# Attention maxima carried to the query rows by DMA from GpSimd's tiles, with queries strided over the score tiles

## The chip, the cores and the metric

The kernel runs on one core of a Trainium2 chip. The metric is device time in microseconds (us) for one launch. Engines are called as the profile calls them: PE (TensorE, with its weight loads as PEld), DVE (VectorE), ACT (ScalarE), POOL (GpSimd), and SP (SyncE), which here only issues DMAs.

## What is computed

A Mamba layer with residual and layer norm, and then a second layer that adds 16-head attention and a top-2 mixture of eight experts, with residual and layer norm. Batch is 8, length 1024, width 256, head width 16. The change touches the attention alone:

```python
qkv = (x @ W_qkv + b_qkv).reshape(B, S, 3, H, hd)
q, k, v = (qkv[:, :, 0], qkv[:, :, 1], qkv[:, :, 2])
attn = jnp.einsum('bqhd,bkhd->bhqk', q, k) / jnp.sqrt(jnp.asarray(hd, x.dtype))
attn = jax.nn.softmax(attn, axis=-1)
attn_out = jnp.einsum('bhqk,bkhd->bqhd', attn, v).reshape(B, S, D)
```

## The kernel before

`mamba_phase` runs first, for all eight batches; `attention_phase` follows and takes the second half of the time. Each engine runs its own instructions in the order in which they are written; semaphores tie them.

For each batch the attention phase has an expert stage (`experts`) and then sixteen head steps (`step(b, h, ...)`). Per head every score is computed twice. First `scores` (L1242) multiplies a 128-query tile `qt` of `q_st`, as the stationary operand, by all 1024 keys, in two halves; DVE's `take_max` (L1623) reduces each tile to the negated row maximum, `neg_max[:, h % 2, qt]`. Later `scores_t` (L1281) multiplies a 128-key tile `kt` of `k_st`, stationary, by the queries of one half, moving. This product has two rows more: `q_st` holds the negated maxima in two float16 parts, `k_st` a constant, so that the maximum is subtracted by the matmul. ACT's `exp_unit` (L1509) turns the result into `probs`, and `weigh_v` (L1296) multiplies these by V.

`q_st` and `k_st` hold each head twice, at partitions 0 and 64. A `scores_t` of one half is issued beside a `scores` of the other half, so the two run in different rows of the PE array.

A step of head h on PE has eight units, kt = 0 to 7. Each issues `scores_t(h, kt, 0)`, `scores(h + 2, kt, 1)`, `scores_t(h, kt, 1)`, `scores(h + 2, kt, 0)` and then `weigh_v`: tiles 4 to 7 of head h - 1 in units 0 to 3, tiles 0 to 3 of head h in units 4 to 7 (LAG = 4). Below, (kt, half) names a `scores_t` or its exponential. Steps 14 and 15 have no `scores`; in their place come parts of the next batch's projections. `turn_o` (L1311), in unit 5, transposes the weighted sums of head h - 1, which ACT's `take_o` (L1516) has copied out of PSUM bank 6; DVE's `normalise` divides them. `weigh_v(h, 0)`, in unit 4, overwrites bank 6 and so waits for `take_o`.

Three PSUM banks (RING = 4, 5, 7) go round among users in a fixed order, the list USERS: the sixteen (kt, half) of a head, `rows` after (3, 1), and `sums` (`turn_o`) after (5, 1). A user waits in `ring_free` until the user three places before it has been read.

The maxima's path from `neg_max` to `q_st`, for head h + 1 during step h:

- POOL, `split_max` (L1193 to L1198): two scalings of `neg_max`, one into float32 `m_rest`, one into float16 `m_hi`; then a copy and a subtraction into the float32 `m_parts`, 128 x 16.
- PE, `turn_max` (L1273), after unit 3: transposes `m_parts` into a ring bank. For head 0 it stands in the expert stage.
- ACT, `take_max` (L1522), after the exponential (4, 0): copies 16 x 128 values to `m_rows`, float16.
- SP, `max_rows` (L1142): four DMAs, each with four runs of 256 bytes from `m_rows` to one row of `q_st`. `scores_t(h + 1, 0, 0)` waits for all four.

Of the kernel before, what the change touches and what calls it, by code (L numbers as in the profile page):

```python
# [916 lines left out]
def attention_phase(nc, d):  # L917
    with ExitStack() as ctx:
# [3 lines left out]
        def sem(name):  # L922
            return ctx.enter_context(nc.semaphore(name))
# [32 lines left out]
        comb_s = sb("comb_s", [P, TT, E])  # L956
        neg_max = sb("neg_max", [P, 2, TT])
        m_rest = sb("m_rest", [P, TT])
        m_hi = sb("m_hi", [P, TT], F16)
        m_parts = sb("m_parts", [P, 2, TT])  # L960
        m_rows = sb("m_rows", [2 * TT, P], F16)

        ones = sb("ones2", [P, P])
        tiny = sb("tiny", [P, 1])
# [76 lines left out]
        s_mx = sem("max_done")  # L1041
        s_ms = sem("max_split_step")
        s_mp = sem("max_parts_done")
        s_mt = sem("max_transposed")
        s_mr = sem("max_rows_ready")
        s_md = sem("max_rows_stacked")
        s_st = sem("scoresT_ready")
        s_p = sem("probs_ready")
        s_vh = sem("v_head_ready")
# [30 lines left out]
        for h in range(HEADS):  # L1080
            for kt in range(TT):
                USERS += [("probs", h, 2 * kt), ("probs", h, 2 * kt + 1)]
                if kt == 3 and h < HEADS - 1:
                    USERS.append(("rows", h + 1, 0))
                if kt == 5 and h:
                    USERS.append(("sums", h - 1, 0))
        SLOT = {user: n for n, user in enumerate(USERS)}
# [8 lines left out]
        def _(sp):  # L1096
# [11 lines left out]
            sp.dma_start(b_vg[:, :], d["b_vg"].broadcast_to([P, GV])).then_inc(s_w, 16)  # L1108
            sp.dma_start(low[:, :, :], d["low"]).then_inc(s_w, 16)
            sp.sem_inc(s_done, 16)  # L1110
            sp.sem_inc(s_md, 16)
            sp.sem_inc(s_qst[0], 16)
            sp.sem_inc(s_qst[1], 16)

# [20 lines left out]

            def max_rows(b, h):

                sp.wait_ge(s_mr, b * HEADS + h + 2)
                for part in range(2):
                    for half in range(2):  # L1140
                        row = half * RG + QR + part
                        sp.dma_start(q_st[row:row + 1, ds(h, 1), half * HALF:(half + 1) * HALF].rearrange("p o (c q) -> p (o c) q", q=P),  # L1142
                                     m_rows[part * TT + half * 4:part * TT + half * 4 + 4, :]).then_inc(s_md, 16)

            def store_out(b):
                sp.wait_ge(s_y, (b + 1) * TT)
# [28 lines left out]
        @block.gpsimd  # L1175
        def _(pool):
            pool.sem_inc(s_pv, TT)
            pool.sem_inc(s_pa, 4)
            pool.memset(ones[:, :], 1.0)
            pool.memset(tiny[:, :], 1e-30)  # L1180
            pool.memset(eps_col[:, :], EPS)
            pool.memset(comb_wide[:, :, :], 0.0)
            pool.memset(k_one[:, :], Q_UP).then_inc(s_const, 1)
            pool.memset(v_h[:, :, HD:VC], 0.0).then_inc(s_const, 1)
            pool.wait_ge(s_const, 2)
            pool.memset(v_h[:, :, HD:HD + 1], 1.0).then_inc(s_const, 1)

            def split_max(b, h):

                g = b * HEADS + h  # L1190
                down = 1.0 / Q_UP
                pool.wait_ge(s_mx, g * TT + (TT + 2))
                pool.tensor_scalar(m_rest[:, :], neg_max[:, h % 2, :], down, None, ALU.mult).then_inc(s_ms, 1)  # L1193
                pool.tensor_scalar(m_hi[:, :], neg_max[:, h % 2, :], down, None, ALU.mult).then_inc(s_ms, 1)
                pool.wait_ge(s_ms, g * 2 + 2)
                pool.wait_ge(s_mr, g + 1)
                pool.tensor_copy(m_parts[:, 0, :], m_hi[:, :]).then_inc(s_mp, 1)
                pool.tensor_tensor(m_parts[:, 1, :], m_rest[:, :], m_hi[:, :], ALU.subtract).then_inc(s_mp, 1)  # L1198

            for b in range(NB):  # L1200

                def add_scaled(i):
                    to = x_in[:, i // 2, :]
                    done = b * EU + 2 * i + 4
                    pool.wait_ge(s_ec, b * (EU // 2) + (i + 1))
                    if i == 6:
                        pool.wait_ge(s_eba, b * 5 + 3)
                    for e in range(2):
                        pool.wait_ge(s_pa, done + e)
                        pool.tensor_tensor(to, to, scaled[:, i % 2, e, :], ALU.add).then_inc(s_pa, 1)  # L1210

                for i in range(LAST // 2):
                    add_scaled(i)
                    if i == 10:
                        split_max(b, 0)
                pool.wait_ge(s_ve, (b + 1) * TT)

                def take_v_head(h, first, last):
                    pool.wait_ge(s_pv, (b * HEADS + h) * TT + last)
                    pool.tensor_copy(v_h[:, first:last, 0:HD], v_all[:, first:last, h * HD:(h + 1) * HD]).then_inc(s_vh, 1)  # L1220

                for h in range(HEADS):
                    if h < HEADS - 1:
                        split_max(b, h + 1)
                    take_v_head(h, 0, 5)
                    take_v_head(h, 5, TT)
                    if h == 0:
                        add_scaled(LAST // 2)

        @block.tensor  # L1230
        def _(pe):
# [5 lines left out]
            def scores(b, h, qt, half):  # L1237

                g = b * HEADS + h
                if half == 1:  # L1240
                    pe.wait_ge(s_mx, g * TT + (qt + 1))
                mm = pe.matmul(ps[:, 2 * (qt % 2) + half, :], head(q_st, half, QR, h, qt * P, P),  # L1242
                               head(k_st, half, QR, h, half * HALF, HALF), start=True, stop=True)
                if half == 0:
                    mm.then_inc(s_sc, 1)

            def ring_free(b, user):


                n = SLOT[user] - len(RING)  # L1250
                if n == -3:
                    used(b, LAST - 3)
                elif n == -2:
                    used(b, LAST - 2)
                elif n == -1:
                    pe.wait_ge(s_mr, b * HEADS + 2)
                else:
                    kind, h, i = USERS[n]
                    if kind == "probs":
                        pe.wait_ge(s_p, (b * HEADS + h) * (2 * TT) + i + 3)  # L1260
                    elif kind == "rows":
                        pe.wait_ge(s_mr, b * HEADS + h + 2)
                    else:
                        pe.wait_ge(s_nm, b * HEADS + h + 2)

            def turn_max(b, h):

                if h:
                    ring_free(b, ("rows", h, 0))
                else:  # L1270
                    pe.wait_ge(s_nm, b * HEADS + 1)
                pe.wait_ge(s_mp, (b * HEADS + h + 1) * 2)
                pe.transpose(ps[0:2 * TT, ring_bank(("rows", h, 0)), 0:P], m_parts[:, :, :].rearrange("p c t -> p (c t)"), ident[:, :]).then_inc(s_mt, 1)  # L1273

            def scores_t(b, h, kt, half):

                g = b * HEADS + h
                if kt == 0 and half == 0:
                    pe.wait_ge(s_md, g * 64 + 80)
                ring_free(b, ("probs", h, 2 * kt + half))  # L1280
                pe.matmul(ps[:, ring_bank(("probs", h, 2 * kt + half)), :], head(k_st, half, QM, h, kt * P, P),  # L1281
                          head(q_st, half, QM, h, half * HALF, HALF), start=True, stop=True).then_inc(s_st, 1)
# [64 lines left out]
            def step(b, h, before, ahead, front):  # L1347


                turned = ahead or h == HEADS - PRE  # L1350
                for kt in range(TT):
                    for half in range(2):
                        scores_t(b, h, kt, half)
# [5 lines left out]
                        expert(b, LAST + kt // 2)  # L1359
                    if kt >= LAG:  # L1360
                        weigh_v(b, h, kt - LAG)
                    if turned and kt == 3:
                        turn_max(b, h + 1)
                    if before and kt == 5:
                        turn_o(b, h - 1)
                    for work, args in front.get(kt, ()):
# [35 lines left out]
            def experts(b):  # L1402
                for t in range(4, TT):
                    v_proj(b, t)
                for t in range(TT):
                    for e2 in range(E // 2):
# [10 lines left out]
                        if u in EARLY:  # L1417
# [3 lines left out]
                                pe.wait_ge(s_eba, (b + 1) * 5)  # L1421
                            for half in range(4):
                                scores(b, unit // TT, unit % TT + half // 2, 1 - half % 2)
                            if unit == TT + 2:
                                turn_max(b, 0)
                    if t == 1:

                        pe.wait_ge(s_cb, b + 1)
# [48 lines left out]
        @block.scalar  # L1477
        def _(act):
            act.sem_inc(s_p, 2)
            act.sem_inc(s_mr, 1)  # L1480
            act.sem_inc(s_o, 1)
            act.preload_act_table(ACT.Ln)
            act.wait_ge(s_const, CONSTS)
# [31 lines left out]
                act.wait_ge(s_ot, g + 1)  # L1515
                act.activation(o_sb[:, :], ps[:, 6, 0:T // QUARTERS], ACT.Copy).then_inc(s_o, 1)  # L1516

            def take_max(b, h):
                g = b * HEADS + h
                act.wait_ge(s_mt, g + 1)  # L1520
                act.wait_ge(s_md, g * 64 + 16)
                act.activation(m_rows[:, :], ps[0:2 * TT, ring_bank(("rows", h, 0)), 0:P], ACT.Copy).then_inc(s_mr, 1)  # L1522

            def scale_expert(b, u):

                i = u // 2
# [4 lines left out]
                                         scale=comb_s[:, u // 4, 2 * (u % 4) + e:2 * (u % 4) + e + 1])  # L1531
                mul.then_inc(s_ec, 1)

            def step(b, h, before, turned):
                for kt in range(TT):
                    for half in range(2):
                        exp_unit(b, h, kt, half)
                        if h == 0 and kt == 3 and half == 0:
                            scale_expert(b, EU - 1)
                        if before and kt == LAG - 1 and half == 1:  # L1540
                            take_o(b, h - 1)
                        if turned and kt == 4 and half == 0:
                            take_max(b, h + 1)

            def heads(b):
                step(b, 0, False, True)
                for h in range(1, HEADS - 1):
                    step(b, h, True, True)
                step(b, HEADS - 1, True, False)
                take_o(b, HEADS - 1)  # L1550

            def inv_std(b):
# [15 lines left out]
            def experts(b, late):  # L1568
# [5 lines left out]
                for u in range(1, LAST, 2):  # L1574
# [5 lines left out]
                        inv_std(late)  # L1580
                    if u in (19, 21, 23, 25) and late is not None:
                        ln_out(late, u - 19, u - 17)
                    if u == 25:
                        take_max(b, 0)

            experts(0, None)
            for b in range(NB - 1):
# [348 lines left out]
```

## Time and profile before

| What | us |
|---|---|
| median of three runs | 3646.37 |
| lowest, highest | 3645.26, 3652.3 |
| the profiled execution | 3649.15 |
| its span between first and last instruction | 3647.3 |

The page of the profile gives engine totals over the span. The start of each `scores_t` in the timeline gives the length of a step: step 0 takes 12.8 to 14.6 us in the eight batches, step 14 takes 16.47 us where another batch follows, and the steps between take 9.93 us with few exceptions. A group's row in the timeline has the start of its first instruction, the time from there to the end of its last, how many there are, and in brackets the idle time of the engine before it with what ended it. A stream of pipelined ACT instructions starts one before the last is done, so single durations add up to more than the stream's.

### The profile page before, as it was taken

Reading aid. Unit: us, or ns where it says so; the run is one execution under the profiler, and the core shown is the slowest. Engines: PE = TensorE matmul, PEld = TensorE weight load, DVE = VectorE, ACT = ScalarE, POOL = GpSimd, SP = SyncE. Lnnn points to the kernel's source line nnn. Section 1 sums busy time; section 2 is a strip of 40 time slices with the busy share of each in tenths; the row PEclk is TensorE's granted clock in tenths of the full one; section 3 lists DMA queues with packets and bytes.
Section 4 is the critical chain, followed back from the end, with each engine's and each line's share of the span. In section 5 each row is a group of like instructions: output and inputs, shape, how many; then the busy total and the mean of one; then the engine's idle time right before and its main releaser. Section 6 shows DMA issues by size and latency. Waiting matters only on the chain.

```text
span 3647.3 us, 119651 instructions
## 1 busy us (share of the span) xinstructions
PE 3445.1 (94%) x52062; PEld 1570.1 (43%) x52062; DVE 3138.9 (86%) x3007; ACT 2503.8 (69%) x3816; POOL 1740.2 (48%) x1562
## 2 busy tenths in 40 slices
PE   7999999999999999999599999999999999999997
PEld 4555555555555555465233323333233332332422
DVE  6898888889888888987698897998979979799796
ACT  4665656666565656664379596895967949779598
POOL 5787878878787887877121311213112121131210
PEclk9999999999999999999799999999999999999999
DMA  4444444444454544443620704207043060340700
GB/s 128 134 121 112 142 112 134 133 134 121 109 146 108 153 117 135 124 117 91 129 36 9 109 2 71 47 2 111 8 64 54 2 105 14 46 72 2 105 2 13
DMA packets 145230, 307.74 MB, mean 84 GB/s; under 512 B 24484, under 2 KB 64068, under 8 KB 144452
## 3 DMA queue, kind: packets, MB, share of 16 engines
q1 hardware_dynamic: 144708, 300.10, 35.7%
q8 instruction: 411, 6.73, 0.8%
q14 instruction: 111, 0.91, 0.1%
HBM read 230.68 MB, written 35.13 MB: 73 GB/s over the span
## 4 chain that ended last, share of the span: by engine, by line
PE 18%; ACT 12%; issue 11%; DVE 10%; DMA 0%; SPq 0%; ACTq 0%; DVEq 0%; POOL 0%
ACT probs L1509 12%; PE ps L1296 6%; PE ps L1281 4%; DVE neg_max L1623 3%; PE ps L1331 2%; PE ps L1398 2%; PE ps L1311 1%; PE ps L1343 1%; DVE acc L1775 1%; PE ps L1242 1%; DVE att L1682 1%; DVE acc L1763 1%; DVE acc L1708 1%; DVE x1T L1605 1%; DVE x1T L1603 1%
## 5 line engine op out<-in xcount | busy, mean ns | idle before, releaser
L346 POOL TENSOR_TENSOR z<-z,c_rep 128x1024 f32<-128x1024 f32 x512 | 1368.7, 2684 | 319.5 <-DVE z L847 311.6
L847 DVE TENSOR_TENSOR_SCAN z<-dA,ps 128x1024 f32<-128x1024 f32 x512 | 1158.1, 2278 | 195.5 <-PE ps L404 144.7
L1509 ACT ACTIVATE probs<-ps,e_scale 128x512 f32<-128x512 f32 x2048 | 1241.2, 702 | 116.2 <-PE ps L1281 113.9
L1623 DVE TENSOR_REDUCE neg_max<-ps 128x1 f32<-128x1024 f32 x1024 | 1187.3, 1215 | 44.3 <-PE ps L1242 43.0
L710 ACT ACTIVATE dA<-rep,a_rep 128x1024 f32<-128x1024 f32 x512 | 565.1, 1142 | 243.7 <-DVE z L847 230.8
L404 PEld LDWEIGHTS ps<-diag,u_t 64*64 64x64 f32 x32768 | 531.0, 135 | 387.0 <-issue 386.5
L1281 PE MATMUL ps<-q_st,k_st 50*128 50x512 f16 x2048 | 632.9, 384 | 31.7 <-ACT probs L1509 28.5
L404 PE MATMUL ps<-diag,u_t 64*64 64x64 f32 x32768 | 598.4, 222 | 59.4 <-DVE z L847 43.3
L1296 PE MATMUL ps<-probs,v_h 128*32 128x256 f32 x8192 | 649.4, 391 | 0.6 <-ACT o_sb L1516 0.6
L1242 PE MATMUL ps<-k_st,q_st 48*128 48x512 f16 x2048 | 600.4, 384 | 7.7 <-DVE neg_max L1623 6.8
L423 PE MATMUL ps<-z,eye 128*64 128x512 f32 x2048 | 497.1, 605 | 0.1
L1210 POOL TENSOR_TENSOR x_in<-x_in,sq_e 128x256 f32<-128x256 f32 x256 | 193.1, 754 | 407.0 <-ACT sq_e L1530 393.5
L1398 PE MATMUL ps<-w_e,x1T 128*128 128x512 f16 x1536 | 358.7, 386 | 17.3 <-DVE acc L1775 14.8
L1281 PEld LDWEIGHTS ps<-q_st,k_st 50*128 50x128 f16 x2048 | 161.1, 93 | 468.6 <-ACT probs L1509 196.7
L1193 POOL TENSOR_SCALAR m_rest<-neg_max 128x8 f32<-128x8 f32 x128 | 31.0, 242 | 669.0 <-DVE neg_max L1623 669.0
L1296 PEld LDWEIGHTS ps<-probs,v_h 128*32 128x32 f32 x8192 | 167.6, 108 | 318.4 <-issue 218.0
L1220 POOL COPY v_h<-v_all 128x80 f32<-128x80 f32 (+1 forms) x256 | 60.0, 236 | 437.6 <-PE ps L1296 437.5
L1530 ACT ACTIVATE sq_e<-ps,comb_s 128x256 f32<-128x256 f32 x256 | 106.4, 471 | 224.8 <-PE ps L1398 169.2
L1398 PEld LDWEIGHTS ps<-w_e,x1T 128*128 128x128 f16 x1536 | 145.1, 99 | 211.6 <-DVE acc L1775 28.7
L423 PEld LDWEIGHTS ps<-z,eye 128*64 128x64 f32 x2048 | 124.6, 136 | 218.5 <-issue 176.5
L1242 PEld LDWEIGHTS ps<-k_st,q_st 48*128 48x128 f16 x2048 | 152.2, 93 | 46.7 <-issue 24.3
L360 PE MATMUL ps<-xT,w_res 128*128 128x512 f32 x256 | 127.0, 618 | 0.0
(183 smaller groups left out, 2875.2 us busy)
## 6 DMA issues: line engine op xcount, KB each, us to landing
c_rep<-c_scratch SPq DMA_DIRECT2D x512, 256.0 KB, 3.9
rep<-delta SPq DMA_DIRECT2D x128, 256.0 KB, 5.5
q_st<-qk_halves SPq DMA_DIRECT2D x192, 128.0 KB, 10.0
k_st<-qk_halves SPq DMA_DIRECT2D x192, 128.0 KB, 10.7
qk_halves<-qk_parts SPq DMA_DIRECT2D x32, 512.0 KB, 10.8
x_nat<-in_x SPq DMA_DIRECT2D x9, 1024.0 KB, 7.2
x_rows<-x_nat SPq DMA_DIRECT2D x9, 1024.0 KB, 7.4
xT<-in_xT SPq DMA_DIRECT2D x8, 1024.0 KB, 7.0
```

Of the source, the lines that this page charges most:

```text
L346: pool.tensor_tensor(z[:, k % ZR, :], z[:, k % ZR, :], c_rep[:, slot, :], ALU.mult).then_inc(s_zc, 1)
L404: mm = pe.matmul(ps[q * QD:(q + 1) * QD, 2 + 2 * (k % 2) + r, i * TB:(i + 1) * TB], u_t[rows, i, m * P + j * QD:m * P + (j + 1) * QD], dia ...
L423: mm = pe.matmul(ps[j * QD:(j + 1) * QD, half, :], eye[:, :], z[:, (grp * QN + j) % ZR, half * HALF:(half + 1) * HALF], start=False, stop= ...
L710: act.activation(dA[:, k % AR, :], rep[:, slot, :], ACT.Exp, scale=a_rep[:, m, j, g:g + 1]).then_inc(s_da, 1)
L847: dve.tensor_tensor_scan(z[:, k % ZR, :], dA[:, k % AR, :], pair(1 + k % 2), 0.0, ALU.mult, ALU.add).then_inc(s_z, 1)
L1210: pool.tensor_tensor(to, to, scaled[:, i % 2, e, :], ALU.add).then_inc(s_pa, 1)
L1242: mm = pe.matmul(ps[:, 2 * (qt % 2) + half, :], head(q_st, half, QR, h, qt * P, P), head(k_st, half, QR, h, half * HALF, HALF), start=True ...
L1281: pe.matmul(ps[:, ring_bank(("probs", h, 2 * kt + half)), :], head(k_st, half, QM, h, kt * P, P), head(q_st, half, QM, h, half * HALF, HAL ...
L1296: mm = pe.matmul(ps[VC * j:VC * (j + 1), 6, 0:n], v_h[:, kt, :], probs[:, kt, j * n:(j + 1) * n], start=(kt == 0), stop=(kt == TT - 1), sk ...
L1398: mm = pe.matmul(ps[:, EBANK[u], :], x1T[:, x, k, t * P:(t + 1) * P], w_e[:, w, k, e2 * 2 * H:(e2 + 1) * 2 * H], start=(i == 0), stop=(i = ...
L1509: act.activation(probs[:, kt, half * HALF:(half + 1) * HALF], ps[:, ring_bank(("probs", h, 2 * kt + half)), :], ACT.Exp, scale=e_scale[:, ...
L1623: dve.tensor_reduce(neg_max[:, h % 2, qt:qt + 1], pair(qt % 2), AX.X, ALU.max, negate=True).then_inc(s_mx, 1)
```

## The change

- POOL writes both parts straight into a float16 `m_parts` with two slots, one for even and one for odd heads: three instructions, the float32 copy is gone. It waits for the DMAs of head h - 2 (`s_md`, now one semaphore for each slot).
- SP's `max_rows` waits for POOL and not for ACT. Each of the four DMAs takes 64 partitions' runs of eight float16 (16 bytes) and writes them behind each other into the row of `q_st`.
- So that eight neighbouring values of a partition are eight neighbouring queries, score tile `qt` now takes the queries qt, qt + 8, qt + 16, ...: the stationary operand of `scores` is read with a step of eight elements (16 bytes) where it was contiguous.
- PE's `turn_max`, ACT's `take_max` and the ring's `rows` user go.
- ACT's `take_o` moves ahead by one exponential: it stood after (3, 1) and stands after (3, 0).

```diff
@@ attention_phase, tiles and ring
-        m_hi = sb("m_hi", [P, TT], F16)
-        m_parts = sb("m_parts", [P, 2, TT])
-        m_rows = sb("m_rows", [2 * TT, P], F16)
+        m_parts = sb("m_parts", [P, 2, 2, TT], F16)
...
-                if kt == 3 and h < HEADS - 1:
-                    USERS.append(("rows", h + 1, 0))
@@ SP, max_rows
-                sp.wait_ge(s_mr, b * HEADS + h + 2)
+                sp.wait_ge(s_mp, b * HEADS + h + 1)
+                rows = P // 2
...
-                        sp.dma_start(q_st[row:row + 1, ds(h, 1), half * HALF:(half + 1) * HALF].rearrange("p o (c q) -> p (o c) q", q=P),
-                                     m_rows[part * TT + half * 4:part * TT + half * 4 + 4, :]).then_inc(s_md, 16)
+                        sp.dma_start(q_st[row:row + 1, h, half * HALF:(half + 1) * HALF].rearrange("p (q c) -> p q c", c=TT),
+                                     m_parts[half * rows:(half + 1) * rows, h % 2, part, :]).then_inc(s_md[h % 2], 16)
@@ POOL, split_max
+                if g >= 2:
+                    pool.wait_ge(s_md[g % 2], g // 2 * 64)
                 pool.tensor_scalar(m_rest[:, :], neg_max[:, h % 2, :], down, None, ALU.mult).then_inc(s_ms, 1)
-                pool.tensor_scalar(m_hi[:, :], neg_max[:, h % 2, :], down, None, ALU.mult).then_inc(s_ms, 1)
+                pool.tensor_scalar(m_parts[:, h % 2, 0, :], neg_max[:, h % 2, :], down, None, ALU.mult).then_inc(s_ms, 1)
                 pool.wait_ge(s_ms, g * 2 + 2)
-                pool.wait_ge(s_mr, g + 1)
-                pool.tensor_copy(m_parts[:, 0, :], m_hi[:, :]).then_inc(s_mp, 1)
-                pool.tensor_tensor(m_parts[:, 1, :], m_rest[:, :], m_hi[:, :], ALU.subtract).then_inc(s_mp, 1)
+                pool.tensor_tensor(m_parts[:, h % 2, 1, :], m_rest[:, :], m_parts[:, h % 2, 0, :], ALU.subtract).then_inc(s_mp, 1)
@@ PE, scores and the first wait of scores_t
-                mm = pe.matmul(ps[:, 2 * (qt % 2) + half, :], head(q_st, half, QR, h, qt * P, P),
+                mm = pe.matmul(ps[:, 2 * (qt % 2) + half, :], q_st[half * RG:half * RG + QR, h, qt:T:TT],
...
-                    pe.wait_ge(s_md, g * 64 + 80)
+                    pe.wait_ge(s_md[g % 2], (g // 2 + 1) * 64)
@@ ACT, step
-                        if before and kt == LAG - 1 and half == 1:
+                        if before and kt == LAG - 1 and half == 0:
                             take_o(b, h - 1)
-                        if turned and kt == 4 and half == 0:
-                            take_max(b, h + 1)
```

The next two pieces are PE's, in an early head step: from unit 3 to the start of unit 5. `q_st,k_st` is `scores_t`, `k_st,q_st` is `scores`, `probs,v_h` is `weigh_v`, and in brackets stand the semaphores waited for. Before:

```order
L1281 MATMUL ps<-q_st,k_st 128x512 [waits probs_ready]
L1242 MATMUL ps<-k_st,q_st 128x512
L1296 MATMUL ps<-probs,v_h 32x256 [waits probs_ready]
L1296 MATMUL ps<-probs,v_h 32x256 x3
L1273 MATMUL ps<-ident,m_parts 16x128 [waits max_parts_done,probs_ready]
L1281 MATMUL ps<-q_st,k_st 128x512 [waits probs_ready]
L1242 MATMUL ps<-k_st,q_st 128x512 [waits max_done]
L1281 MATMUL ps<-q_st,k_st 128x512 [waits probs_ready]
L1242 MATMUL ps<-k_st,q_st 128x512
L1296 MATMUL ps<-probs,v_h 32x256 [waits o_taken,v_head_ready,probs_ready]
L1296 MATMUL ps<-probs,v_h 32x256 x3
L1281 MATMUL ps<-q_st,k_st 128x512 [waits max_rows_ready]
```

The same place on PE now:

```order
L1264 MATMUL ps<-q_st,k_st 128x512 [waits probs_ready]
L1236 MATMUL ps<-k_st,q_st 128x512
L1279 MATMUL ps<-probs,v_h 32x256 [waits probs_ready]
L1279 MATMUL ps<-probs,v_h 32x256 x3
L1264 MATMUL ps<-q_st,k_st 128x512 [waits probs_ready]
L1236 MATMUL ps<-k_st,q_st 128x512 [waits max_done]
L1264 MATMUL ps<-q_st,k_st 128x512 [waits probs_ready]
L1236 MATMUL ps<-k_st,q_st 128x512
L1279 MATMUL ps<-probs,v_h 32x256 [waits o_taken,v_head_ready,probs_ready]
L1279 MATMUL ps<-probs,v_h 32x256 x3
L1264 MATMUL ps<-q_st,k_st 128x512 [waits probs_ready]
```

The turn is gone, and the first `scores_t` of unit 5 waits for an exponential where it waited for ACT's copy of the maxima.

ACT, from one head's exponentials to the next head's. Before:

```order
L1509 ACTIVATE probs<-ps,e_scale 128x512 [waits pv_tile_done,scoresT_ready] x15
L1516 ACTIVATE o_sb<-ps 128x256 [waits o_transposed,pv_tile_done]
L1509 ACTIVATE probs<-ps,e_scale 128x512 [waits pv_tile_done,scoresT_ready]
L1522 ACTIVATE m_rows<-ps 16x128 [waits max_rows_stacked,max_transposed]
L1509 ACTIVATE probs<-ps,e_scale 128x512 [waits pv_tile_done,scoresT_ready] x15
```

The same place on ACT now:

```order
L1486 ACTIVATE probs<-ps,e_scale 128x512 [waits pv_tile_done,scoresT_ready] x16
L1493 ACTIVATE o_sb<-ps 128x256 [waits o_transposed,pv_tile_done]
L1486 ACTIVATE probs<-ps,e_scale 128x512 [waits pv_tile_done,scoresT_ready] x16
L1493 ACTIVATE o_sb<-ps 128x256 [waits o_transposed,pv_tile_done]
L1486 ACTIVATE probs<-ps,e_scale 128x512 [waits pv_tile_done,scoresT_ready] x16
```

Ahead of the copy stand seven of a head's exponentials now, and nine behind it; before it was eight and eight, and the copy of the maxima came one later.

## Rows read from the trace of the kernel before

**Rows 1.** The page, first line.

```profile
span 3647.3 us, 119651 instructions
```

**Rows 2.** Stages: length, busy PE, PEld, DVE, ACT, POOL, clock share, DMA share, GB/s.

```profile
2549.90:2679.10 129.20, 126.66 (x1287) 37.80 (x1287) 124.54 (x131) 126.40 (x235) 15.67 (x78) 1.00 0.03 10
...
2717.10:2768.10 51.00, 47.90 (x234) 19.11 (x231) 47.79 (x89) 21.78 (x51) 21.89 (x32) 0.97 0.80 108
```

**Rows 3.** Timeline of ACT over one head step, from the exponential (7, 0) on.

```profile
2569.15 5.89 ACT L1509 ACTIVATE probs<-ps,e_scale 128x512 f32<-128x512 f32 x10
2574.86 0.45 ACT L1516 ACTIVATE o_sb<-ps 128x256 f32<-128x256 f32 x1
2575.13 0.77 ACT L1509 ACTIVATE probs<-ps,e_scale 128x512 f32<-128x512 f32 x1
2575.70 0.25 ACT L1522 ACTIVATE m_rows<-ps 16x128 f16<-16x128 f32 x1
2575.85 1.87 ACT L1509 ACTIVATE probs<-ps,e_scale 128x512 f32<-128x512 f32 x3
2577.93 3.00 ACT L1509 ACTIVATE probs<-ps,e_scale 128x512 f32<-128x512 f32 x5 [0.21 <-PE ps L1281]
```

**Rows 4.** Timeline of PE over the same head step, from unit 0 to the next.

```profile
2569.84 0.39 PE L1281 MATMUL ps<-q_st,k_st 50*128 50x512 f16 x1
...
2570.07 0.38 PE L1281 MATMUL ps<-q_st,k_st 50*128 50x512 f16 x1
...
2570.95 0.39 PE L1281 MATMUL ps<-q_st,k_st 50*128 50x512 f16 x1
...
2573.16 0.39 PE L1281 MATMUL ps<-q_st,k_st 50*128 50x512 f16 x1
...
2573.70 0.64 PE L1296 MATMUL ps<-probs,v_h 128*32 128x256 f32 x8
2574.27 0.28 PE L1273 MATMUL ps<-ident,m_parts 128*16 128x128 f32 x1
2574.52 0.39 PE L1281 MATMUL ps<-q_st,k_st 50*128 50x512 f16 x1
...
2575.10 0.39 PE L1281 MATMUL ps<-q_st,k_st 50*128 50x512 f16 x1 [0.19 <-ACT probs L1509]
...
2576.03 0.39 PE L1281 MATMUL ps<-q_st,k_st 50*128 50x512 f16 x1
...
2577.14 0.44 PE L1311 MATMUL ps<-ident,o_sb 128*128 128x128 f32 x2
2577.51 0.39 PE L1281 MATMUL ps<-q_st,k_st 50*128 50x512 f16 x1
...
2577.77 0.39 PE L1281 MATMUL ps<-q_st,k_st 50*128 50x512 f16 x1
...
2578.66 0.39 PE L1281 MATMUL ps<-q_st,k_st 50*128 50x512 f16 x1
...
2579.77 0.39 PE L1281 MATMUL ps<-q_st,k_st 50*128 50x512 f16 x1
```

**Rows 5.** Timeline of DVE over the same head step.

```profile
2569.49 5.74 DVE L1623 TENSOR_REDUCE neg_max<-ps 128x1 f32<-128x1024 f32 x5
2575.56 2.38 DVE L1623 TENSOR_REDUCE neg_max<-ps 128x1 f32<-128x1024 f32 x2 [0.34 <-PE ps L1242]
```

**Rows 6.** Groups of weight loads: stationary*moving shape, count, busy us, mean ns, idle before.

```profile
L1242 PEld LDWEIGHTS ps<-k_st,q_st 48*128 48x128 f16 x2048 | 152.2, 93 | 46.7 <-issue 24.3 <-DVE neg_max L1623 20.8
L435 PEld LDWEIGHTS ps<-w_io,s_res 128*128 128x128 f32 x512 | 93.3, 190 | 14.0
```

**Rows 7.** The maxima's path: POOL's last part, SP's issues, another transfer of short runs.

```profile
2571.45 0.20 POOL L1198 TENSOR_TENSOR m_parts<-m_rest,m_hi 128x8 f32<-128x8 f32 x1
...
2575.97 2.42 SPq L1142 DMA_DIRECT2D q_st<-m_rows  x4
...
w_dt<-in_b_dt SPq DMA_DIRECT2D x4, 0.5 KB, 2.1
```

**Rows 8.** Timeline of PE, first matmul of step 1 in the same batch.

```profile
2550.01 0.39 PE L1281 MATMUL ps<-q_st,k_st 50*128 50x512 f16 x1 [0.22 <-DMA q_st<-m_rows]
```

More of the change, by code:

```diff
@@ L1043, in attention_phase @@
         s_mp = sem("max_parts_done")
-        s_mt = sem("max_transposed")
-        s_mr = sem("max_rows_ready")
-        s_md = sem("max_rows_stacked")
+        s_md = (sem("max_rows_stacked_even"), sem("max_rows_stacked_odd"))
         s_st = sem("scoresT_ready")
@@ L1110, in _ @@
             sp.sem_inc(s_done, 16)
-            sp.sem_inc(s_md, 16)
             sp.sem_inc(s_qst[0], 16)
@@ L1255, in ring_free @@
                 elif n == -1:
-                    pe.wait_ge(s_mr, b * HEADS + 2)
+                    used(b, 3)
                 else:
@@ L1260, in ring_free @@
                         pe.wait_ge(s_p, (b * HEADS + h) * (2 * TT) + i + 3)
-                    elif kind == "rows":
-                        pe.wait_ge(s_mr, b * HEADS + h + 2)
                     else:
                         pe.wait_ge(s_nm, b * HEADS + h + 2)
[L1266 to L1273, printed above, removed]
             def scores_t(b, h, kt, half):
@@ L1347, in step @@
             def step(b, h, before, ahead, front):
-                turned = ahead or h == HEADS - PRE
                 for kt in range(TT):
@@ L1361, in step @@
                         weigh_v(b, h, kt - LAG)
-                    if turned and kt == 3:
-                        turn_max(b, h + 1)
                     if before and kt == 5:
@@ L1423, in experts @@
                                 scores(b, unit // TT, unit % TT + half // 2, 1 - half % 2)
-                            if unit == TT + 2:
-                                turn_max(b, 0)
                     if t == 1:
@@ L1479, in _ @@
             act.sem_inc(s_p, 2)
-            act.sem_inc(s_mr, 1)
             act.sem_inc(s_o, 1)
@@ L1516, in take_o @@
                 act.activation(o_sb[:, :], ps[:, 6, 0:T // QUARTERS], ACT.Copy).then_inc(s_o, 1)
[L1518 to L1522, printed above, removed]
             def scale_expert(b, u):
@@ L1532, in scale_expert, with step @@
                 mul.then_inc(s_ec, 1)
-            def step(b, h, before, turned):
+            def step(b, h, before):
                 for kt in range(TT):
@@ L1539, in step @@
                             scale_expert(b, EU - 1)
-                        if before and kt == LAG - 1 and half == 1:
+                        if before and kt == LAG - 1 and half == 0:
                             take_o(b, h - 1)
-                        if turned and kt == 4 and half == 0:
-                            take_max(b, h + 1)
             def heads(b):
-                step(b, 0, False, True)
+                step(b, 0, False)
                 for h in range(1, HEADS - 1):
-                    step(b, h, True, True)
-                step(b, HEADS - 1, True, False)
+                    step(b, h, True)
+                step(b, HEADS - 1, True)
                 take_o(b, HEADS - 1)
@@ L1582, in experts @@
                         ln_out(late, u - 19, u - 17)
-                    if u == 25:
-                        take_max(b, 0)
             experts(0, None)
```

## The prediction, made before the changed kernel was run

> **What bounds the kernel now.** The first line of the page gives the span, 3647.3 us [rows 1]; the profiled execution took 3649.15, so 1.9 us lie around it, and it is 2.8 us above the median of 3646.37. I take what the sum gives off the median. The Mamba half is untouched. The table of stages splits one batch of the attention half [rows 2]: thirteen ordinary head steps take 129.2 us, of which PE is busy 126.7, ACT 126.4 and DVE 124.5. No engine alone is the bound; three run close to each other, and what each loses comes from waiting in turn. The expert stage (51.0 us) is led by PE, busy 47.9.
>
> So I read one step in the timelines. It lasts 2579.77 - 2569.84 = 9.93 us [rows 4]. ACT: ten exponentials take 5.89 us and five take 3.00, so one more costs 0.578 and a lone one 0.69 [rows 3]. The run ends at 2575.04, and (4, 0), with `take_o` in between, ends at 2575.90: the copy costs 0.86 - 0.578 = 0.28. Sixteen exponentials and this copy make 9.53, the least ACT can do after the change. ACT idles 0.21 ahead of (6, 0). DVE idles 0.34 per step, ahead of tile 4 [rows 5], so its least is 9.59. PE: a unit is 1.11 (2569.84 to 2570.95), `turn_o` 0.37 (2577.14 to 2577.51), `turn_max` 0.25 (2574.27 to 2574.52) [rows 4]. Without `turn_max` PE needs 8 x 1.11 + 0.37 = 9.25.
>
> Where PE waits: (4, 1) comes 0.58 after (4, 0), where a pair follows its neighbour after 0.23 elsewhere; it could start only when (3, 1)'s exponential had ended, at 2575.04, and started 0.06 later. The ring does this: with `rows` in it, (4, 1) stands three places behind (3, 1). Then ACT does two copies, PE does `turn_o`, and ACT idles for it.
>
> **The step after the change.** I set unit 0 at 0 and go through it with these durations: an exponential ends 0.578 after the one before, or 1.11 after the start of its `scores_t` if that comes later (2577.51 to 2577.93, and 0.69); a `scores_t` starts 0.05 after the end of the exponential three places before. E is the end of an exponential, S the start of a `scores_t`. Up to unit 3 nothing changes: E(3, 0) = 5.20 - 0.58 = 4.62, S(3, 0) = 3.32.
> - `take_o` now follows (3, 0), but must also wait for the last `weigh_v` of head h - 1, which ends at 2574.34, or 4.50 [rows 4]. With 0.04 to react and at least 0.38 for the copy (0.45 in this row, started behind other work [rows 3]) it ends at 4.92; behind (3, 0) alone it would be 4.90. So E(3, 1) = 5.50, E(4, 0) = 6.08, E(4, 1) = 6.65, E(5, 0) = 7.23, E(5, 1) = 7.81.
> - `turn_max` gone: S(4, 0) = 4.43; (4, 1) now waits for (3, 0): 4.67 (5.26 before). `weigh_v(h, 0)` could start at 4.99 and `take_o` lets it go at 4.97. S(5, 0) = 5.56. But (5, 1) now stands behind (4, 0): 6.13, not 5.79. **The ring's wait moves from unit 4 to unit 5** and shrinks from 0.35 to 0.34: hardly at all.
> - `turn_o` 7.01, S(6, 0) = 7.38, E(6, 0) = 8.49. (6, 1) waits for (5, 1): 7.86. S(7, 0) = 8.74, E(7, 0) = 9.85, next unit 0 at 9.85, E(0, 0) 11.01, that is 1.16 into the step, as it is now. The step closes on itself at **9.85**, 0.08 less.
>
> So what is removed, 0.25 on PE and some 0.15 on ACT (2575.70 to 2575.85), comes through by a third: ACT still idles for (6, 0) and now for (7, 0), since the ring of three lets PE no further ahead. DVE has its tile 4 about 0.4 earlier and gives the time back at tiles 5 and 6. 13 steps x 8 batches x 0.08 = **8.6 us**.
>
> **Other places.** Step 0 loses `turn_max` and the wait of step 1 for the maxima's DMA, 0.22 [rows 8]; step 14, bound by PE, and the expert stage lose a `turn_max` each: 0.22 + 3 x 0.25 = 0.97 per batch, **8 us** in all. From below nothing of it need show, if DVE or ACT takes it back; from above step 0 could gain some 0.5 more.
>
> **The maxima's path.** Before, SP issues at 2575.97, four DMAs in 2.42 us; now it can when POOL is done, at 2571.65 or 0.2 earlier [rows 7]. The nearest row for short runs is `b_dt` into `w_dt`: 128 runs of 4 bytes, landed in 2.1 us. 1.8 to the last issue and 2.1 give 2575.6; the rows are needed at 2579.77, so over 4 us cover it, and even twice the issue time and twice the landing only reach that point. POOL's new wait is for DMAs of a step before the last. SP has nothing else between maxima except the next batch's stacks, which come after head 15's maxima as before. Cost 0; if the cover were gone, each step would be late by the excess.
>
> **The strided stationary operand.** Its cost is in no row. A weight load of 128 float16 columns takes 93 ns, one of 128 float32 columns 190 [rows 6]. Say a load gets longer by x. Not all is hidden: a pair starts 0.23 after the pair ahead, but `weigh_v`, which must replace the weights of all rows, 0.31 after it (2573.70 less 2573.16 and 0.23) [rows 4]. The first `scores` load of a unit follows `weigh_v` and is exposed in the same way, the second lies under a matmul. Bounds for x: 0 and 97 ns. I take 0, nearer to the row of its own size and type, since the column count stays; but it is the weakest step here.
>
> On this the row shows only that 128 contiguous columns take 93 ns. The Trainium skill speaks against the change: SBUF — State Buffer, in the note on cachelines in its part on the DMA port swizzle, says that a line has 16 bytes and that each access crossing to a new line pays a penalty, unless a line is hit twice; here every column is in another line. It states no price, and would make x positive. TensorE: Matmul & The Clock Gate, Weight-path perf modes, lets the fast load read its columns "packed or strided", which would make x 0. No row here decides between them.
>
> **Sum.** 8.6 + 8 = 16.6 off the median: 3629.8, say **3630 us**, the forecast, with its own range 3618 to 3638.
>
> **Rivals.**
> 1. Slower: the strided load costs x in each unit. The loop that then decides runs from (7, 0) through units 0 to 3 to the end of `weigh_v`, `take_o`, five exponentials, (6, 1) and (7, 0) again, and has six exposed loads, with 0.02 us of slack: 9.85 + 6x. With 24 more in each batch (16 expert-stage pairs, 8 units of step 0) the total is 104 x 6x + 192x = 816x. It cancels the gain at x = 20 ns; at 50 ns it adds 41: **3671**; at 97 ns, 3709. For it: the access changes, `take_o` moved onto PE's `weigh_v`, and PE has no air in units 0 to 3. Against: nothing is added in column count.
> 2. The wait only moves: the step stays 9.93 and one `turn_max` in the expert stage and one in step 14 remain as gain, 2 x 8 x 0.25 = 4 us: **3642**. For it: my step's gain is 0.08 out of terms rounded to 0.02. Against: two pieces of work are gone from the loop.
> 3. The engines fall into a better phase and a step reaches DVE's least, 9.59: 0.34 x 104 = 35, with the 8: **3603**. Against: the ring keeps its three banks and (6, 1) still waits for (5, 1).
>
> **Chances.** Forecast 0.49, rival 1 with over 29 ns 0.27, rival 1 between 11 and 29 ns or rival 2 0.18, rival 3 0.06. This kernel's runs tell about 0.2%, 7.3 us, from no change; forecast and rival 3 lie below that, with bits of the third case above it at either side: faster 0.53, same 0.19, slower 0.28. The range leaves out rival 3 and rival 1 beyond some 55 ns: 3615 to 3675.
>
> **What would show it.** Right: steps of 9.85 us; no idle before (4, 1), a wait of about 0.34 at (5, 1); ACT idle at (6, 0) and (7, 0); `scores` weight loads of 93 ns; DMAs of the maxima issued 4 us earlier and nobody waiting for them. Wrong: units 0 to 3 longer than 1.11 us, or longer `scores` loads (rival 1); SP issues much over 0.6 us each, or unit 0 waiting for a DMA; the forecast also fails if `take_o` ends later than 4.92, as ACT then carries that into every step.

## The result and the profile after

The changed kernel takes 3664.45 us (median of five runs, 3661.24 to 3670.12) against 3646.37: a ratio of 1.0045, 95% interval 1.0033 to 1.0056. It is slower: by 16 us by the ratio, by 18 between the medians. The forecast was 3630. One of the twelve executions of a later kernel (e5) took 12268.6 us at a mean granted clock of 0.504, its others 3640 to 3658; its ratio leaves that one out.

The page of the changed kernel, the span and the engines' busy time:

```profile
span 3662.7 us, 118872 instructions
...
PE 3483.5 (95%) x51934; PEld 1597.5 (44%) x51934; DVE 3164.7 (86%) x3007; ACT 2514.6 (69%) x3688; POOL 1720.9 (47%) x1434
```

The span of before is in [rows 1]. There are 128 matmuls and 128 ACT instructions fewer, and the span is 15.4 us longer. The weight loads of `scores`, in the columns of [rows 6]:

```profile
L1236 PEld LDWEIGHTS ps<-k_st,q_st 48*128 48x128 f16 x2048 | 190.2, 141 | 48.6 <-issue 24.8 <-DVE neg_max L1590 22.5
```

**141 ns where there were 93.** PE over one head step of the changed kernel (line 1264 is `scores_t`, 1294 `turn_o`), to lay beside [rows 4]:

```profile
2596.20 0.39 PE L1264 MATMUL ps<-q_st,k_st 50*128 50x512 f16 x1
2596.47 0.38 PE L1264 MATMUL ps<-q_st,k_st 50*128 50x512 f16 x1
2597.35 0.39 PE L1264 MATMUL ps<-q_st,k_st 50*128 50x512 f16 x1
...
2599.66 0.39 PE L1264 MATMUL ps<-q_st,k_st 50*128 50x512 f16 x1
...
2600.82 0.39 PE L1264 MATMUL ps<-q_st,k_st 50*128 50x512 f16 x1
2601.10 0.38 PE L1264 MATMUL ps<-q_st,k_st 50*128 50x512 f16 x1
2602.05 0.39 PE L1264 MATMUL ps<-q_st,k_st 50*128 50x512 f16 x1
2602.55 0.39 PE L1264 MATMUL ps<-q_st,k_st 50*128 50x512 f16 x1
2603.49 0.44 PE L1294 MATMUL ps<-ident,o_sb 128*128 128x128 f32 x2
2603.86 0.39 PE L1264 MATMUL ps<-q_st,k_st 50*128 50x512 f16 x1
2604.28 0.39 PE L1264 MATMUL ps<-q_st,k_st 50*128 50x512 f16 x1
2605.22 0.39 PE L1264 MATMUL ps<-q_st,k_st 50*128 50x512 f16 x1
...
2606.38 0.39 PE L1264 MATMUL ps<-q_st,k_st 50*128 50x512 f16 x1
```

The second pair follows the first by 0.28 us, not 0.23, and the next unit follows the second pair by 0.88 as before: a unit is 1.16 and not 1.11. Two of its loads are longer by 48 ns each, and it grows by the length of one. (4, 1) no longer waits, 0.28 after (4, 0). (5, 1) follows (5, 0) by 0.50, and (6, 1) follows (6, 0) by 0.42. The step is 10.18 us here, and 10.19 as the median of the 104 steps, against 9.93.

ACT and DVE over the same step, beside [rows 3] and [rows 5]:

```profile
2595.46 5.32 ACT L1486 ACTIVATE probs<-ps,e_scale 128x512 f32<-128x512 f32 x9
2600.95 0.38 ACT L1493 ACTIVATE o_sb<-ps 128x256 f32<-128x256 f32 x1 [0.17 <-PE ps L1279]
2601.23 5.68 ACT L1486 ACTIVATE probs<-ps,e_scale 128x512 f32<-128x512 f32 x9
```
```profile
2595.76 7.00 DVE L1590 TENSOR_REDUCE neg_max<-ps 128x1 f32<-128x1024 f32 x6
2603.02 1.23 DVE L1590 TENSOR_REDUCE neg_max<-ps 128x1 f32<-128x1024 f32 x1 [0.25 <-PE ps L1236]
```

ACT's wait ahead of (6, 0) is too short to stand in brackets, and there is a new one of 0.17 us ahead of the copy: the copy waits for `weigh_v`. The waits of the whole kernel say how often:

```profile
ACT o_sb L1493 <- PE ps L1279: 25.5, 104, 1.1
```

That is 104 times: once in each of steps 2 to 13, and in each batch at the copy that follows step 15, which already waited up to 1.1 us in the kernel before. In step 1 the copy finds no idle time ahead of it. The maxima's path over one step, POOL's last part and SP's issues, and the row of transfers with its median time to landing, beside [rows 7]:

```profile
2587.41 0.20 POOL L1192 TENSOR_TENSOR m_parts<-m_rest,m_parts 128x8 f16<-128x8 f32 x1
...
2587.64 3.02 SPq L1136 DMA_DIRECT2D q_st<-m_parts  x4
...
q_st<-m_parts SPq DMA_DIRECT2D x512, 1.0 KB, 1.8
```

SP has issued all four at 2590.66, a transfer lands 1.8 us after its issue, and the rows are needed at 2596.20.

### The profile page after: what moved, and what is told of

Same layout as the page of the kernel before. It is cut to its first block, busy times and chain, and to the rows that moved or that the text cites. A ratio compares the mean times of both kernels' runs of the same rounds, so it can differ in the third digit from the quotient of the medians.

```text
span 3662.7 us, 118872 instructions
## 1 busy us (share of the span) xinstructions
PE 3483.5 (95%) x51934; PEld 1597.5 (44%) x51934; DVE 3164.7 (86%) x3007; ACT 2514.6 (69%) x3688; POOL 1720.9 (47%) x1434
## 4 chain that ended last, share of the span: by engine, by line
PE 34%; DVE 11%; issue 4%; ACT 3%; DMA 0%; DVEq 0%; ACTq 0%; POOL 0%; SPq 0%
PE ps L1279 14%; PE ps L1264 11%; PE ps L1236 4%; DVE neg_max L1590 3%; ACT probs L1486 3%; PE ps L1314 2%; PE ps L1378 2%; PE ps L1294 1%; PE ps L1326 1%; DVE acc L1742 1%; DVE acc L1730 1%; DVE att L1649 1%; DVE acc L1675 1%; DVE x1T L1572 1%; DVE x1T L1570 1%
## 5 line engine op out<-in xcount | busy, mean ns | idle before, releaser
L1590 DVE TENSOR_REDUCE neg_max<-ps 128x1 f32<-128x1024 f32 x1024 | 1204.6, 1220 | 36.4 <-PE ps L1236 28.1
L1264 PE MATMUL ps<-q_st,k_st 50*128 50x512 f16 x2048 | 673.8, 383 | 8.0 <-DMA q_st<-m_parts 0.2
L1236 PE MATMUL ps<-k_st,q_st 48*128 48x512 f16 x2048 | 640.7, 414 | 6.9 <-DVE neg_max L1590 6.4
L1378 PE MATMUL ps<-w_e,x1T 128*128 128x512 f16 x1536 | 356.9, 385 | 16.6 <-DVE acc L1742 14.6
L1236 PEld LDWEIGHTS ps<-k_st,q_st 48*128 48x128 f16 x2048 | 190.2, 141 | 48.6 <-issue 24.8
## 6 DMA issues: line engine op xcount, KB each, us to landing
q_st<-qk_halves SPq DMA_DIRECT2D x192, 128.0 KB, 10.1
```

Of the source, the lines that this page charges most:

```text
L1236: mm = pe.matmul(ps[:, 2 * (qt % 2) + half, :], q_st[half * RG:half * RG + QR, h, qt:T:TT], head(k_st, half, QR, h, half * HALF, HALF), st ...
L1378: mm = pe.matmul(ps[:, EBANK[u], :], x1T[:, x, k, t * P:(t + 1) * P], w_e[:, w, k, e2 * 2 * H:(e2 + 1) * 2 * H], start=(i == 0), stop=(i = ...
L1590: dve.tensor_reduce(neg_max[:, h % 2, qt:qt + 1], pair(qt % 2), AX.X, ALU.max, negate=True).then_inc(s_mx, 1)
```

## The experiments

The theory from this profile (A, later C): the 16-byte step makes each `scores` load 48 ns longer, one load per unit is exposed, and the copy's new place, behind the end of `weigh_v`, brings six such units into the loop that sets the step. Rivals: the short DMA runs or the moved copy alone (B), and the stride alone, wherever the copy stands (D).

Totals are medians beside runs of the kernel before on the same chip, whose medians were 3646.37 us beside the changed kernel, 3651.03 beside e1 to e4, 3650.19 beside e5 to e8 and 3652.62 beside e9 to e12; so the ratios are to be compared, not the totals. Step is the median of the 104 head steps 1 to 13, from starts of `scores_t` in the profiled execution; in e4 and e12, the same kernel, it is 9.91 both times. The total also carries the Mamba half, which took from 1841.9 us (changed) to 1859.5 us (e6) in the profiled executions. Load is the mean of a `scores` weight load.

| Kernel | Load, ns | Step, us | Total, us | Ratio to before, 95% |
|---|---|---|---|---|
| before | 93 | 9.93 | | |
| changed | 141 | 10.19 | 3664.45 | 1.0045 (1.0033 to 1.0056) |
| e1, before with the stride | 142 | 10.03 | 3658.66 | 1.0022 (1.0012 to 1.0032) |
| e2, changed without the stride | 93 | 9.90 | 3633.44 | 0.9952 (0.9935 to 0.9968) |
| e3, changed with step 4 | 110 | 10.01 | 3653.38 | 1.0006 (0.9996 to 1.0015) |
| e4, changed with step 2 | 93 | 9.91 | 3637.67 | 0.9965 (0.9953 to 0.9978) |
| e5, changed, copy late | 142 | 9.99 | 3649.9 | 0.9995 (0.9983 to 1.0008) |
| e6, step 2, copy late | 93 | 9.94 | 3642.75 | 0.9979 (0.9969 to 0.9990) |
| e7, no stride, copy late | 93 | 9.94 | 3639.84 | 0.9980 (0.9967 to 0.9993) |
| e8, before, copy early | 93 | 10.22 | 3682.04 | 1.0080 (1.0062 to 1.0099) |
| e9, step 2, turn beside late copy | 93 | 9.61 | 3606.55 | 0.9876 (0.9860 to 0.9893) |
| e10, the same, copy early | 93 | 9.88 | 3631.83 | 0.9944 (0.9928 to 0.9960) |
| e11, stride, turn beside late copy | 141 | 9.62 | 3609.79 | 0.9883 (0.9865 to 0.9900) |
| e12, e4 again | 93 | 9.91 | 3641.3 | 0.9964 (0.9953 to 0.9976) |

### The stride alone (e1)

```diff
-head(q_st, half, QR, h, qt * P, P)
+q_st[half * RG:half * RG + QR, h, qt:T:TT]
```

> The kernel before with the strided stationary operand alone; maxima still travel by PE's turn, ACT's copy and 256-byte runs, and so reach other queries than those they belong to (the step from tile to row order is left out). Theory A (the 16-byte step of the weight load is the whole loss): scores loads go from 93 to about 141 ns, units 0 to 2 of a head step from 1.11 to 1.16 us, the step from 9.93 to between 10.0 and 10.3 us, the kernel 8 to 35 us slower than before. Theory B (the short DMA runs into q_st, or the copy moved ahead, are the loss): loads and steps stay at 93 ns and 9.93 us, no change.

The strided load by itself makes the kernel before slower, and its loads and units are those of the changed kernel. But a step grows by 0.10 only, though eight units grow by 0.05 each: most of it goes into the time in which (4, 1) waited in the ring anyway: (4, 0) comes 0.15 us later in the step than before, and (4, 1), which waits for ACT, 0.04 earlier.

### All but the stride (e2)

The same edit in reverse, on the changed kernel.

> The changed kernel with a contiguous stationary operand; the maxima again reach other queries than their own. Theory A: loads 93 ns, step 9.85 us, about 16 us faster than before, near 3630. Theory B: loads 93 ns but the step stays near 10.19 us and the kernel near 3664.

Theory B falls: with the short DMA runs, the new ring and the early copy, but without the stride, the kernel is faster than before. ACT in one step, whose 0.17 us of idle time ahead of the copy is gone:

```profile
2583.64 5.32 ACT L1486 ACTIVATE probs<-ps,e_scale 128x512 f32<-128x512 f32 x9
2588.90 0.38 ACT L1493 ACTIVATE o_sb<-ps 128x256 f32<-128x256 f32 x1
2589.18 5.63 ACT L1486 ACTIVATE probs<-ps,e_scale 128x512 f32<-128x512 f32 x9
```

And PE in the same step, the last `weigh_v` ahead of the copy, (6, 1) and (7, 0):

```profile
2588.19 0.64 PE L1279 MATMUL ps<-probs,v_h 128*32 128x256 f32 x8
...
2592.23 0.39 PE L1264 MATMUL ps<-q_st,k_st 50*128 50x512 f16 x1
...
2593.12 0.39 PE L1264 MATMUL ps<-q_st,k_st 50*128 50x512 f16 x1
```

The copy is still tied to the end of `weigh_v` (2588.83, and it starts at 2588.90), but that end comes sooner. (7, 0) follows the waiting pair (6, 1) by 0.89 us here and by 0.94 in the changed kernel (2604.28 to 2605.22): after a wait the second pair's own load is exposed. With the five units 7 and 0 to 3 that is the sixth longer load in the loop.

### Steps of four and two (e3, e4)

```diff
-q_st[half * RG:half * RG + QR, h, qt:T:TT]
+q_st[half * RG:half * RG + QR, h, qt // 4 * HALF + qt % 4:(qt // 4 + 1) * HALF:4]        # e3
+q_st[half * RG:half * RG + QR, h, qt // 2 * 2 * P + qt % 2:(qt // 2 + 1) * 2 * P:2]      # e4
```

POOL's parts go out by DMA to match: runs of 8 bytes from 128 partitions, four DMAs per head (e3), or runs of 4 bytes, eight DMAs per head (e4). Every maximum reaches its own query in both.

> The changed kernel with a step of four elements (8 bytes): tile qt takes every fourth query of one half; each DMA moves 128 runs of 8 bytes. If the cost is that no two columns share 16 bytes: loads back at 93 ns, step 9.85 us, near 3630, faster than both. If any step above one element costs: loads near 141 ns, near 3664.

> The same with a step of two elements (4 bytes), runs of 4 bytes and eight DMAs per head in place of four (5 to 6 us of issue per step of 9.9). If the cost is per 16 bytes: loads 93 ns, as step 4 or slightly slower where SP is late, 3630 to 3640. If any step costs: loads near 141 ns, near 3664. A size between the two in both kernels would mean a cost that grows with the step.

The loads of `scores` with the stride alone, with step 4 and with step 2:

```profile
L1242 PEld LDWEIGHTS ps<-k_st,q_st 48*128 48x128 f16 x2048 | 181.5, 142 | 40.1 <-issue 21.7 <-DVE neg_max L1623 18.0
```
```profile
L1235 PEld LDWEIGHTS ps<-k_st,q_st 48*128 48x128 f16 x2048 | 183.8, 110 | 49.5 <-DVE neg_max L1589 25.1 <-issue 23.4
```
```profile
L1237 PEld LDWEIGHTS ps<-k_st,q_st 48*128 48x128 f16 x2048 | 163.7, 93 | 50.4 <-issue 25.9 <-DVE neg_max L1591 22.9
```

Both my readings for e3 missed: the load is neither 93 nor 141. The cost grows with the step, 93, 93, 110 and 141 ns for one, two, four and eight elements of two bytes. Six times 17 ns on the 9.90 us of e2 make 10.00, and e3's step is 10.01: the loop holds at this size too. The Trainium skill (SBUF — State Buffer, note on cachelines) names lines of 16 bytes and asks for two hits on each; it was right in that eight elements cost, but step 4 still has two hits per line and cost 17 ns here. The same note gives eight bf16 as the step that is free, which the loads of 141 ns contradict for float16. e4 takes the maxima along the changed kernel's path, with a step of two in place of eight and twice the DMAs, and is faster than both kernels; e12, the same kernel again, gives the same ratio.

### The place of the copy (e5 to e8)

```diff
-                        if before and kt == LAG - 1 and half == 0:
+                        if before and kt == LAG - 1 and half == 1:
```

e5, e6 and e7 are the changed kernel, e4 and e2 with this edit; e8 is the kernel before with its reverse.

> The changed kernel, stride and all, with take_o back behind the exponential (3, 1). Theory C (the copy's new place ties ACT to the end of weigh_v in unit 3, so that six lengthened units come into the step): the copy then ends at the end of (3, 1) plus 0.28 and is not bound to PE; the loop that remains runs over 11 exponentials, the copy, weigh_v of unit 4, units 5 and 6 and has one exposed strided load, 9.90 us; the kernel about 30 us below the changed one, near 3634. Theory D (the stride alone sets 10.19 us, wherever the copy stands): 10.1 to 10.3 us, no gain or a loss, since unit 5 starts later by 0.2 us.

> Step of two elements with take_o behind (3, 1). Theory C: without lengthened loads the two places are within 0.05 us of each other, a step of 9.85 against 9.91, 0 to 6 us less than with the early copy. Theory D: no gain, or slower because weigh_v of unit 4 waits for a later copy.

> Contiguous stationary operand (maxima reach other queries than their own) with take_o behind (3, 1). Theory C: 9.85 us against 9.90 with the early copy, near 3630. Theory D: 9.90 or more.

> The kernel before with take_o moved ahead to stand behind (3, 0), nothing else. (3, 1) then ends at 5.6 instead of 5.2 us into the step, and (4, 1), which waits for it in the ring, starts at 5.7 instead of 5.26: Theory C: 10.2 to 10.3 us per step, 30 to 38 us slower than before. Theory D: 9.93 us, no change.

With the new path for the maxima, the four corners are:

| Step, us | copy behind (3, 0) | copy behind (3, 1) |
|---|---|---|
| contiguous | 9.90 | 9.94 |
| step of eight | 10.19 | 9.99 |

The stride costs 0.29 us with the early copy and 0.05 with the late one. 0.29 is six times 48 ns, as the loop says. Theory D falls by e5, whose step it put at 10.1 to 10.3. My own numbers were off as well: e5's step is 9.99, not 9.90, and its total is level with the kernel before, some 18 us by the ratios below the changed one and not 30; and e6 and e7 are slower than with the early copy, not faster, as D had it. One term accounts for both, seen in e5 on PE (line 1279 is `weigh_v`) and in ACT's copy:

```profile
2591.57 0.38 ACT L1493 ACTIVATE o_sb<-ps 128x256 f32<-128x256 f32 x1
```
```profile
2592.10 0.64 PE L1279 MATMUL ps<-probs,v_h 128*32 128x256 f32 x8 [0.30 <-ACT o_sb L1493]
```

The copy ends at 2591.95 and the waiting `weigh_v` starts 0.15 later, where I had used 0.05, the figure for a `scores_t` that waits for an exponential. With 0.10 more, the loop of e5 gives 10.00 and those of e6 and e7 9.95. Why this restart takes longer no run here shows.

e8 came out as expected. With `rows` still in the ring, (4, 1) waits for (3, 1), and the early copy delays just that:

```profile
2611.84 0.39 PE L1281 MATMUL ps<-q_st,k_st 50*128 50x512 f16 x1 [0.52 <-ACT probs L1509]
```

So the early copy gains only in a ring without `rows` between (3, 1) and (4, 1), and there 0.04 us (e2 against e7), and only while units are short.

### The turn beside the copy (e9 to e11)

If the step is set by PE waiting for ACT's copy and then ACT waiting for PE's turn, the two should be taken apart. PE now turns head h - 2 after unit 3, where ACT copies head h - 1, so the turn no longer waits for the copy of its own step. e9 is e6 with this edit, e10 is e4 and e11 is e5 with it:

```diff
-                if kt == 5 and h:
-                    USERS.append(("sums", h - 1, 0))
+                if kt == 3 and h >= 2:
+                    USERS.append(("sums", h - 2, 0))
+                if kt == 5 and h == HEADS - 1:
+                    USERS.append(("sums", h - 1, 0))
...
-        o_sb = sb("o_sb", [P, T // QUARTERS])
+        o_sb = sb("o_sb", [P, 2, T // QUARTERS])
...
-                act.wait_ge(s_ot, g + 1)
+                act.wait_ge(s_ot, g)
...
-                    if before and kt == 5:
-                        turn_o(b, h - 1)
+                    if h >= 2 and kt == 3:
+                        turn_o(b, h - 2)
+                    if h == HEADS - 1 and kt == 5:
+                        turn_o(b, h - 1)
...
-                    if qt == 5 and before:
-                        normalise(b, h - 1)
+                    if qt == 3 and h >= 2:
+                        normalise(b, h - 2)
```

> Step of two elements, take_o behind (3, 1), and turn_o of head h - 2 (not h - 1) on PE after unit 3, so that PE turns while ACT copies; o_sb has two slots, normalise moves along. Theory C (the step is set by loops in which PE waits for ACT's copy and ACT then waits for PE's turn, one after the other): the loop left is E(5, 0), 13 exponentials, the copy 0.28, 0.15 to restart PE, weigh_v 0.57, and 1.11: 9.62 us per step, close to DVE's 9.59; about 29 us below the step-2 kernel, near 3610. Theory D (PE's own work bounds the step): 9.9 us as before.

> The same with take_o behind (3, 0). With sums in the ring after (3, 1), (4, 1) waits for (3, 1), which the copy and the end of weigh_v delay to 5.53: about 9.8 us per step, 10 us below the step-2 kernel. Theory D: 9.9 us.

> The changed kernel (step of eight elements, loads of 141 ns, four DMAs of 64 runs) with take_o behind (3, 1) and turn_o beside the copy. Theory C: no exposed load lies on the loop of 9.62, but PE's own work becomes 8 x 1.16 + 0.39 = 9.67 us: 9.65 to 9.75 us per step, some 50 us below the changed kernel. Theory D: 10.0 or more.

> The step-2 kernel with take_o behind (3, 0) once more, beside the three above: 9.91 us per step, 0.2 to 0.5% below the kernel before; the step length should not move, the total by a few us with the part ahead of the attention.

e9 has a step of 9.61 us, 0.01 from the loop as worked out, and the kernel is the fastest of all, 46 us below the one before. ACT over one step of e9, and then PE around the copy (1491 is `exp_unit`, 1498 the copy, 1297 the turn, 1267 `scores_t`):

```profile
2571.95 5.90 ACT L1491 ACTIVATE probs<-ps,e_scale 128x512 f32<-128x512 f32 x10
2577.64 0.48 ACT L1498 ACTIVATE o_sb<-ps 128x256 f32<-128x256 f32 x1
2577.90 4.94 ACT L1491 ACTIVATE probs<-ps,e_scale 128x512 f32<-128x512 f32 x8
```
```profile
2577.06 0.44 PE L1297 MATMUL ps<-ident,o_sb 128*128 128x128 f32 x2
2577.43 0.39 PE L1267 MATMUL ps<-q_st,k_st 50*128 50x512 f16 x1
2577.91 0.39 PE L1267 MATMUL ps<-q_st,k_st 50*128 50x512 f16 x1
```

ACT has no idle time in brackets any more. The turn ends at 2577.50, before the copy starts at 2577.64, so the two do not run at the same time; what has gone is the turn's wait for that copy. The agreement with the loop is not proof of the loop alone: DVE's least was 9.59 us, and e9 cannot tell a step set by the loop from one set by DVE.

e10 was expected at 9.8 and took 9.88, with `sums` standing where `rows` stood in e8; this is too near to theory D's 9.9 to speak against it. e9 and e11 do. e11 is the strongest word against the stride as the whole story: its loads take 141 ns and its units 1.16 us, as in the changed kernel, and its step is 9.62, within 0.01 of the step-2 version. PE over one step of e11 (1266 is `scores_t`, 1296 the turn):

```profile
2580.02 0.39 PE L1266 MATMUL ps<-q_st,k_st 50*128 50x512 f16 x1
...
2584.65 0.44 PE L1296 MATMUL ps<-ident,o_sb 128*128 128x128 f32 x2
2585.02 0.39 PE L1266 MATMUL ps<-q_st,k_st 50*128 50x512 f16 x1
...
2589.65 0.39 PE L1266 MATMUL ps<-q_st,k_st 50*128 50x512 f16 x1
```

Four units, the turn and four units follow each other without a wait: 4.63, 0.37 and 4.63 us. Here PE's own work sets the step, and it happens to be as long as the loop of e9. So a still longer load should show at once; no run shows it.

## Why the prediction was wrong

**The step that failed is the strided stationary operand**, where I took x = 0 as "nearer to the row of its own size and type" [rows 6]. It is 48 ns. e1 has the step alone, on the kernel before, and its loads take 142 ns; e2 is without it, on the changed kernel, and gains. Nothing in the trace of before had a step in it, and the row that I preferred differs from the case in the very thing that was changed. With x = 0.048 my own loop gives 9.85 + 0.29 = 10.14 and a total of 3629.8 + 816 x 0.048 = 3669; measured were 10.19 and 3664. Rival 1 happened, almost at the 50 ns for which I had put 3671, and I had given it 0.27. The 3664 lie inside my range of 3615 to 3675, but the range took in a gain and a loss alike. The loop's share of rival 1, six loads per step, was right. The 192x for the rest, 9 us, was not: from e2 to the changed kernel step 0 grows by 0.05 us, the stretch from step 15 to the next step 0 by 0.09 in its shorter form, and step 14 not at all, about 1 us in eight batches.

**The step without the stride** was right in its shape: the wait at (4, 1) goes (4.68 into the step in e2, I had 4.67), one comes at (5, 1) (6.16, I had 6.13), one is left at (6, 1) (7.90, I had 7.86), and the gain is a small part of what was removed. The size was 9.90, not 9.85. The copy starts 0.07 after `weigh_v` has ended and not 0.04, and the rest is rounding: the five exponentials behind it take 2.90 and not 2.89, and (7, 0) follows (6, 1) by 0.89 and not 0.88. That the copy lets PE go after 0.15 and not 0.05 costs nothing here, since it delays only (5, 0), and (5, 1) waits for ACT anyway. So the gain is 104 x 0.034 = 3.5 us, where I had 8.6 (and 104 x 0.08 is 8.3).

**Other places**: I had 8 us. Step 0 went from 13.03 to 12.60 us in its median (e2), 3.4 us in eight batches. Step 1 went from 10.03 to 10.09, so the two together gave 0.37 and not the 0.47 forecast. Step 14 went from 16.47 to 16.44, and the expert stage with step 15 stayed at 71.1 us, so its turn had been hidden. In the profiled executions of the changed kernel and of before the attention half differs by 17.3 us: steps 2 to 13 give +23.2, step 1 +1.6, step 0 -6.4, the rest -1.1. Of step 0's, 3.1 come from two batches of before in which it took 14.6 us; in the one that starts at 2768.08 the granted clock was 0.50 from 2777.3 to 2780.7, with matmuls of 0.6 us.

**The total without the stride** came near the forecast by luck. e2 is 17.5 us below before by its ratio, and I had 16.6, but not by my terms: its attention half is 15.5 us shorter in the profiled executions, of which steps 2 to 13 give 4.4, step 0 7.3 with the two slow ones of before, and the stretches from step 15 to step 0 4.4, which are longer in four of seven cases in before and in one in e2 (see the last section).

**The maxima's path** was right: cost 0. In the whole changed kernel PE waits for these transfers once, 0.2 us. A transfer lands in 1.8 us where 2.1 was assumed, and over 3 us of cover are left with the longer issues, 3.02 us for four against 2.42.

**The place of the copy** I had treated as a term in the step and named in rival 1. What I had not seen is that the stride's price hangs on it: the early copy cost nothing by itself (9.90 against 9.94) and made the stride six times as dear (0.29 against 0.05). Rival 2 did not happen. Rival 3's length, 9.59, was not reached by this change, but e9 came within 0.02 of it, by moving work and not by removing it.

## What to carry to other kernels

Where a tile is laid out so that a DMA writes long rows, look at who reads it with a step: as a stationary operand, float16 with a step of two cost nothing here, four cost 17 ns and eight 48 ns per load, while the short DMA runs cost the steps nothing that could be seen. When three engines are nearly full, write down the loops of waits and count how often the lengthened piece occurs in each; the same 48 ns cost 0.29, 0.10, 0.05 or nearly 0 us per step by the place of a copy, a turn or a user of the ring. And before taking work out of such a loop, see whether two waits that follow each other can be taken apart.

## What was not expected of the hardware

The load time against the step (93, 93, 110, 141 ns) is one. The other is the granted clock in the stretch from step 15 to the next batch's step 0, which lasted 71.1 to 71.4 us or 1.4 to 1.6 us more, both forms in every kernel. Two such stretches of the kernel before, in the columns of [rows 2]:

```profile
2695.60:2768.10 72.50, 69.31 (x424) 29.61 (x420) 59.62 (x112) 33.12 (x71) 22.37 (x34) 0.98 0.81 111
3159.60:3230.60 71.00, 67.81 (x423) 29.53 (x419) 58.91 (x112) 33.10 (x71) 22.59 (x34) 1.00 0.84 113
```

The work is the same; the mean granted clock is 0.98 in one and 1.00 in the other. In the longer one the granted clock was 0.50, the level of 1.2 GHz, from 2749.98 to 2753.40 us. The longer form came in four of seven stretches of before, three of the changed kernel, one of e2 and five of e3. Such differences come to 6 us between two totals, and a comparison of steps avoids them. What decides it no run here shows, nor whether a change has a part in it: there is one profiled execution of each kernel.
